# Four graph layers on one core: source keys first, masks on two engines, ranking by one scan per 32 columns

## What is computed

```
edge_index = stack([src, dst])
x = layernorm(x + segment_sum(h[dst], src))          # layer 0: h = x @ W.T + b
x = layernorm(x + layer1(x))                         # agg = segment_sum(h[src], dst), then an MLP, norm, relu
x = layernorm(x + layer2(x))                         # agg = segment_sum(weight * x[dst], src), two BN stages
x = layernorm(x + attention(x, edge_attr_128))       # softmax over the edges of one src
```

## Time and profile before

| | us |
|---|---|
| time, median of 3 runs | 6961.44 (6958.57 to 6962.66) |
| span of the profiled execution | 5494.9 |
| difference of the two | 1466.5 |
| GpSimd busy | 3860.8 (70% of the span) |
| VectorE busy | 3566.7 (65%) |
| TensorE busy | 3536.2 (64%) |
| ScalarE busy | 1431.3 (26%) |
| scatter DMAs issued (800) | from 108.3 to 1147.3 |

### The profile page before, as it was taken

One profiled execution on the slowest core, in us unless ns is written; L12 is line 12 of the kernel. 1 busy time (PEld: TensorE's weight loads), 2 busy tenths in 40 slices (PEclk: granted clock), 3 DMA queues, 4 the chain that ended last, 5 costly groups with the idle time before them and its releaser, 6 DMA issues.

```text
span 5494.9 us, 71163 instructions
## 1 busy us (share of the span) xinstructions
PE 3536.2 (64%) x14107; PEld 2622.1 (48%) x14107; DVE 3566.7 (65%) x11740; ACT 1431.3 (26%) x4459; POOL 3860.8 (70%) x4043
## 2 busy tenths in 40 slices
PE   2878694135555555566666656566666578888887
PEld 2655462024444444455555534444444445555554
DVE  8888887335555555566666645555554667788887
ACT  0211110000000000000000022222224456777776
POOL 2777777777777777777777667777773077777774
PEclk8999896567778777888888878877778789999999
DMA  3323231023333333333333333333331133343334
GB/s 86 82 70 78 64 89 37 2 71 112 111 111 112 111 113 104 107 113 111 113 111 112 100 98 105 105 105 105 105 105 49 51 106 109 111 113 111 112 112 75
DMA packets 257376, 521.07 MB, mean 95 GB/s; under 512 B 88217, under 2 KB 128621, under 8 KB 257139
## 3 DMA queue, kind: packets, MB, share of 16 engines
q0 software_dynamic: 179984, 423.92, 27.6%
q1 hardware_dynamic: 77155, 94.66, 5.9%
HBM read 483.72 MB, written 34.57 MB: 94 GB/s over the span
## 4 chain that ended last, share of the span: by engine, by line
PE 36%; POOL 17%; DMA 17%; issue 12%; DVE 12%; ACT 4%; DVEq 2%; SPq 0%; ACTq 0%; POOLq 0%
PE ps L1213 21%; POOL ZT L690 12%; DMA ZT<-table,meta_src 9%; POOL rec_src L635 5%; DMA ZT<-table,meta_dst 5%; PE ps L1223 3%; PE ps L1208 3%; DMA ACC<-in_edge_attr 2%; DVE ZT L1695 2%; PE ps L1172 2%; PE ps L1228 2%; DVE meta_src L1730 2%; DVE X L2117 1%; PE ps L1380 1%; DVE meta_src L1733 1%
## 5 line engine op out<-in xcount | busy, mean ns | idle before, releaser
L690 POOL DMA_INDIRECT ZT<-table,meta_dst x1616 | 1542.1, 954 | 684.7 <-issue 337.8
L690 POOL DMA_INDIRECT ZT<-table,meta_src x1568 | 1485.0, 947 | 513.8 <-issue 323.0
L1213 PE MATMUL ps<-ZT,xT 128*128 128x256 f32 x4704 | 1528.3, 496 | 467.7 <-DMA ZT<-table,meta_src 309.9
L1213 PEld LDWEIGHTS ps<-ZT,xT 128*128 128x128 f32 x4704 | 1215.2, 261 | 789.2 <-issue 179.7
L1812 DVE TENSOR_TENSOR ACC<-ps,ACC 128x256 f32 x2352 | 997.9, 424 | 813.4 <-PE ps L1213 553.8
L635 POOL DMA_INDIRECT rec_src<-ZT x800 | 796.4, 995 | 329.2 <-issue 239.1
L1208 PE MATMUL ps<-ZT,sel_x 128*128 128x256 f32 x294 | 162.6, 652 | 700.4 <-DMA ZT<-table,meta_src 495.9
L2117 DVE SCALAR_TENSOR_TENSOR X<-X,corr,ps 128x256 f32 x832 | 397.7, 478 | 134.5 <-PE ps L1223 47.2
L1172 PE MATMUL ps<-ewW,xT 128*128 128x256 f32 x1600 | 454.5, 386 | 0.0
L1223 PE MATMUL ps<-ZT,xT 128*128 128x256 f32 x1664 | 403.9, 393 | 50.7 <-ACT xT L965 21.5
L1208 PEld LDWEIGHTS ps<-ZT,sel_x 128*128 128x128 f32 x294 | 65.8, 279 | 751.4 <-DMA ZT<-table,meta_src 283.6
(11 more groups left out here) (423 smaller groups left out, 4530.9 us busy)
## 6 DMA issues: line engine op xcount, KB each, us to landing
ACC<-in_edge_attr SPq DMA_DIRECT2D x200, 240.0 KB
ZT<-table,meta_dst POOLq DMA_INDIRECT x1616
ZT<-table,meta_src POOLq DMA_INDIRECT x1568
rec_src<-ZT POOLq DMA_INDIRECT x800
table<-X SPq DMA_DIRECT2D x98, 128.0 KB
table<-ZT SPq DMA_DIRECT2D x49, 128.5 KB
table<-z SPq DMA_DIRECT2D x12, 512.0 KB
out<-X SPq DMA_DIRECT2D x48, 128.0 KB
```

Of the source, the lines that this page charges most:

```text
L690: pool.indirect_dma_start(rows[:, s % depth, 0:width], None, table[layer], bass.IndirectOffsetOnAxis(ap=ids[:, s, 0:1].bitcast(I32), axis= ...
L1213: nc.tensor.matmul(slot_sum(j), sel[:, k % 2, j, :], ring[:, (2 + k) % RG * G + j, 0:D], start=True, stop=True).then_inc(sem["summed"], 1)
```

## The change

**Loads.** SP waits for one memset in place of five and loads the source keys first, under a semaphore of their own (`src_in`). The next-partition words, the destination keys and the weights come behind; the node rows `X` come in one DMA behind the small loads and the first four steps of edge features.

**Masks.** VectorE makes masks 0 to 26 (`MARKED`). GpSimd makes masks 27 to 49 (`RANKED` is 50: the last stands for the empty partitions), and ScalarE counts them (`count_marks`). The copies of keys and weights into the records move from VectorE to ScalarE (`copy_pay`, `copy_list`).

**Ranks.** For each round's 32 columns (`RN`), ScalarE copies 50 masks by 32 columns to floats, laid out tile by tile with one place ahead of each tile (`open_steps`). VectorE puts each tile's base in that place and scans the whole line of 50 x 33 = 1650 in one instruction; a row of bytes (`going`) that is 0 at the head of each tile starts the sum anew. The last place of each tile is the next round's base. A product with the masks and a sum over the tiles leave the ranks of 32 columns. There are 25 such rounds: the first ahead of the edge work, the others each behind a round of it. The destination keys keep the old way (`rank_dst`), which does not run on these inputs.

**First layer's rows.** A pair of tiles in each of the 25 rounds: TensorE turns them after the third step of a round and multiplies after the sixth, in PSUM banks 6 and 7.

```diff
+RN = SC * SG
+MARKED = 27
+RANKED = T + 1
...
+            sp.wait_ge(sem["zeroed"], 1)
+            load_row(key[0], a["src"], sem["src_in"])
+            sp.wait_ge(sem["zeroed"], 4)
+            load_row(key[1], a["dst"], sem["keys_in"])
+            load_row(weight_row, a["edge_weight"], sem["keys_in"])
...
+            load_attr(0, 0, AR)
+            sp.wait_ge(sem["pool_set"], 1)
+            sp.dma_start(X[:, 0:T - 1, :], a["x"][0:(T - 1) * P, :].rearrange("(t p) d -> p t d", p=P)).then_inc(sem["x_in"], 16)
...
+            pool.wait_ge(sem["bucket_ready"], 1)
+            for b in range(MARKED, RANKED):
+                pool.tensor_scalar(mask[:, b, :], bucket, float(b if b < T else NO_NODE // P), None,
+                                   ALU.is_equal).then_inc(sem["marked"], 1)
...
-                    if c % (SC * SG) == 0 and c // (SC * SG) in BLOCKS:
-                        pool.wait_ge(sem["record_ready"], BLOCKS.index(c // (SC * SG)) + 1)
+                    if c % RN == 0:
+                        pool.wait_ge(sem["record_ready"], c // RN + 1)
+                        pool.wait_ge(sem["pay_set"], 3 if c == 0 else 6)
...
+            def count_marks(b):
+                act.wait_ge(sem["marked"], b - MARKED + 1)
+                nc.scalar.activation(mask[:, b, :], mask[:, b, :], ACT.Copy,
+                                     accum_out=small[:, 0, b:b + 1]).then_inc(sem["counted"], 1)
+
+            def open_steps(i):
+                c = slice(i * RN, (i + 1) * RN) if isinstance(i, int) else bass.ds(i * RN, RN)
+                wait(act, sem["record_ready"], i)
+                nc.scalar.copy(steps[:, :, 1:RN + 1], mask[:, :, c]).then_inc(sem["step_ready"], 1)
...
-                with dve.Fori(0, T) as b:
+                with dve.Fori(0, MARKED if n == 0 else T) as b:
...
-            def rank_block(which, block, c0, c1):
-                base = (which * (len(BLOCKS) - 1) + block) * T
                 for b in range(T):
-                    wait(dve, sem["ranked"], base + b - 1)
...
-                    v.tensor_tensor_scan(run[b % 2][:, c0:c1], ones[:, 0:1].to_broadcast([P, c1 - c0]), mask[:, b, c0:c1],
-                                         small[:, 5, b:b + 1], ALU.mult, ALU.add).then_inc(sem["scanned"], 1)
...
+            def rank_src(i):
...
+                own = steps[:, :, 1:RN + 1]
+                dve.wait_ge(sem["step_ready"], i + 1)
+                step(1, v.tensor_copy(steps[:, :, 0], rank_base[:, :]))
+                step(2, v.tensor_tensor_scan(step_line, going, step_line, 0.0, ALU.mult, ALU.add))
+                step(3, v.tensor_copy(rank_base[:, :], steps[:, :, RN]))
+                step(4, v.tensor_tensor(own, own, mask[:, :, c], ALU.mult))
+                step(5, v.tensor_reduce(found_rows, own.rearrange("p t c -> p c t"), AX_X, ALU.add))
+                v.tensor_copy(rec_of[0][:, c], found_rows).then_inc(sem["record_ready"], 1)
...
             edge_round(0)
-            for block in range(1, len(RANK_AT)):
-                with dve.Fori(max(RANK_AT[block - 1], 1), RANK_AT[block]) as i:
-                    edge_round(i)
-                rank_src(block)
...
+            rank_src(1)
+            with dve.Fori(1, SITERS - 1) as i:
                 edge_round(i)
+                rank_src(i + 1)
+            edge_round(SITERS - 1)
```

More of the change, by code:

```diff
@@ L182, in ring_group_3, with edge_rounds, last_round @@
     return b, u * RG + k
[L185 to L189, removed]
+def edge_rounds(eng, edge_round):
+    edge_round(0)
+    with eng.Fori(1, SITERS - 1) as i:
         edge_round(i)
-    edge_round(end - 1, last=True)
+    edge_round(SITERS - 1)
+def last_round(i):
+    return isinstance(i, int) and i == SITERS - 1
 def each_batch(body, first=0, end=NB):
@@ L299, in gnn_program @@
         row_from = small[:, 3, :]
+        rank_base = small[:, 3:5, :].rearrange("p i t -> p (i t)")[:, 0:RANKED]
         one_hot = cslot[0:T, 0:SLOTS]
@@ L742, in _ @@
             nc.scalar.activation(a_relu, a_relu, ACT.Copy, scale=1.0 - SLOPE).then_inc(sem["w_ready"], 1)
+            for b in range(half, T):
+                count_marks(b)
+            act.wait_ge(sem["marked"], RANKED - MARKED)
+            act.wait_ge(sem["counted"], T)
+            open_steps(0)
             act.wait_ge(sem["ew_psum"], 2)
@@ L1173, in edge_z, with edge_round @@
                 mm.then_inc(sem["ez_psum"], 1)
[L1175 removed]
+            def edge_round(i):
                 for u in range(ES):
[L1178 removed]
+                    if not (last_round(i) and u == ES - 1):
                         turn_attr(i, u + 1)
                     edge_z(i, u)
[L1181 to L1188 removed]
+                    if u == 2:
+                        if isinstance(i, int) and i == 0:
+                            pe.wait_ge(sem["w_ready"], 3)
+                            pe.wait_ge(sem["x_in"], 48)
+                        first_columns(i)
+                    if u == 5:
+                        first_rows(i)
+            pe.wait_ge(sem["split_ready"], 2)
+            pe.wait_ge(sem["zeroed"], 7)
+            pe.wait_ge(sem["pool_set"], 1)
+            turn_attr(0, 0)
+            for i in range(SITERS):
+                edge_round(i)
+            pe.wait_ge(sem["y_used"], NJ)
             order_tiles(0)
@@ L1706, in rank_src @@
-            def rank_src(block):
-                rank_block(0, block, BLOCKS[block] * SC * SG, BLOCKS[block + 1] * SC * SG)
+                    link(v.tensor_tensor_scan(run[0], ones[:, 0:1].to_broadcast([P, COLS]), mask[:, b, :],
+                                              small[:, 5, b:b + 1], ALU.mult, ALU.add))
+                    link(v.copy_predicated(pos, mask[:, b, :], run[0]))
+                v.tensor_copy(rec_of[1], pos).then_inc(sem["record_ready"], 1)
+                dve.wait_ge(sem["record_ready"], SITERS + 1)
@@ L1753, in _ @@
             order_slots_3()
+            dve.wait_ge(sem["keys_in"], KEYS_IN)
+            dve.wait_ge(sem["x_in"], 48)
             tile_counts(1, 1)
-            bases()
+            bases(small[:, 5, :])
             with dve.If(read_order(dve) > 0):
```

248 lines of the change are left out of this document (136 added, 112 removed).

## The result

| measured together, each line in one set on one chip | kernel before, us | changed kernel, us | ratio, 95% interval |
|---|---|---|---|
| the result | 6960.0 | 6835.0 | 0.983 [0.981, 0.985] |
| both once more | 6947.6 | 6848.3 | 0.985 [0.982, 0.988] |
| both in a later set | 5501.7 | 5550.0 | 1.009 [1.007, 1.010] |

A forecast was written before the change was run, and what follows sets the result against it. GpSimd was taken as the bound: first scatter at 56, plus 1017 + 10 + 91 = 1118 us, puts the last at 1174 against 1147.3, +26. So 6961.4 + 26 = 6988 us, range 6955 to 7020 (8 in 10).

The forecast's parts named there:

- The base: Whole time: span 5494.9 us, with 1466.5 us up to the median left as they are; the forecast adds 26 to 6961.4.
- what VectorE saves after 108 is hidden: Scatter stage: GpSimd's first scatter and its pace over 800 set the end, so VectorE's later savings gain nothing.
- VectorE becomes the bound: Rival, rank rounds: over 20.6 us each, VectorE decides; at 24 us, 7070 us. Chance 0.10, shared with a late start.
- First scatter at 56: Start of the stage: shorter loads, masks and first ranks bring the first scatter 52 us sooner, bounds 50 to 73.
- the bound not chosen: GpSimd's masks at the start: 2.12 us each by the two-input price, so done at 58 and first scatter at 73.
- Hold of the scatters: Rank rounds: scan (2.9 us) and product (0.85 us) hold GpSimd's scatters, 3.8 us a round, 91 us over 24.
- does not grow: Rival, rank rounds: the hold does not lengthen with the instruction, 24 rounds cost 11 us, time 6908 us. Chance 0.17.
- only the scan holds: Rival, rank rounds: the product holds no scatter, 70 us instead of 91, 6967 us. Chance 0.18, including anything between.
- Scatter's own pace: GpSimd's scatters when not held: 1.273 us each, 0.97 and 0.30 of issue, 1017 us for the stage.
- VectorE idle over 100 us before the read-back: End of the stage: sign that the forecast is right, VectorE having finished its work before the scatters end.
- Nothing changes behind the read-back: After the scatter list is read back: everything behind 1150.49 is untouched and only moves with the stage's end.
- the forecast of +26 us: End of the scatters: last scatter at 1174 against 1147.3, carried unchanged into the whole time.

The follow-up runs named there:

- the second trace of the changed kernel: The changed kernel, unchanged, profiled once more, with stops: 6848.3 us; the kernel before took 6947.6 us.

## Why the prediction was wrong, by its own steps

**The base, and with it the bound: the step that failed.** "The profile has the span, 5494.9, and 1466.5 us lie between it and the median; no row shows them and I leave them as they are." They do not lie outside the span: in every later run the time is 2 us above the span of the same execution. The trace was of an execution without stops, the median of runs with them, and the prediction applied the bound of the first to the time of the second. Where the result was measured, "what VectorE saves after 108 is hidden" is false: GpSimd waits 497 us for edge sums in the kernel before (412 of them behind its first scatter), and what shortens the edge stage counts. The prediction took the end of the old blocks at 12 us of scatters and the new rank rounds at 91; measured at the edge steps, which are the path there, they are 152 and 58. By the trace alone this could not be seen, but a gap of 1466.5 us that no row explains was a reason to give this case a chance of its own, with the edge steps as the bound already in the kernel before. The rival "VectorE becomes the bound" asked only whether the changed kernel crosses a threshold, and put it on the slower side.

The other steps can be read where their premise holds, without stops:

- **First scatter at 56, bounds 50 to 73: it is 76.8.** GpSimd's mask was taken at 1.03 us, and measured 2.21; the bound not chosen (2.12) was the right one. The prediction's own text gives a 58 for that; TensorE's sum starts at 57.7. ScalarE's count was taken at 1.25 and is 0.87, with 0.18 more to read its sum out. The first rank round takes 11.2 us, not 8.2: the sum over the tiles, priced by a row of 800 elements side by side at 1.8, takes 2.98 when it walks rows with a stride, and 1.9 us are the bias split's, of which the prediction said that it "comes behind and costs nothing" (see the run with all masks on VectorE).
- **Hold of the scatters, 91 us: right, at 86.** The two scatters that meet a scan and a product are 86 us above the median over the 24 rank rounds. All 800 are 800 x (1072 - 958) ns = 91 us above it, against 800 x (995 - 969) = 21 before; the forecast had 91 + 10. The rivals "does not grow" and "only the scan holds" fall by the timeline of the rank round.
- **Scatter's own pace:** 958 ns in place of 969, 9 us less over 800, not foreseen. With 5.8 us of waits for edge sums behind the first scatter: 76.8 + 1102.5 = 1179.3, where 1174 was forecast (56 + 1118). That the two lie so near is in part luck: a start 21 us later than forecast against a stretch 15 us shorter.
- **VectorE idle over 100 us before the read-back: 64.2.** The longer sum, 24 x 1.2 = 29 us, and longer rounds. The edge steps end at 959, not 866.
- **Nothing changes behind the read-back: wrong by 15 us.** The span grows by 47.1 and the scatter's end only by 32.0. The gathers of the last layer, in a line that the change does not touch, without stops, before and then after:

```profile
L690 POOL DMA_INDIRECT ZT<-table,meta_dst x832: 942/946/1484, 4389.8 to 5439.7; - x167
```

```profile
L720 POOL DMA_INDIRECT ZT<-table,meta_dst x832: 952/957/1737, 4427.0 to 5485.7; - x167
```

Each takes 11 ns more, some 9 us over 832. The other 6 come up in the second layer, between its first gather (+31.1) and the third layer's (+37.1). I have no cause for either, and no run was made for it.

So without stops the forecast of +26 us stands against +32 at the end of the scatters and +48 in the time. The sign was right there and wrong where it was asked.

## What the runs showed of the hardware

- **Stops.** In some sets VectorE, ScalarE, TensorE and SP are held again and again in dense stretches (an edge round of 51.6 us where 23.7 are enough), GpSimd was not seen held in this stage, and the same kernel takes 26% longer (6948 to 5498 us). Stretches with little work for TensorE are nearly free of them: the edge steps' end to the memset of `ACC` takes 159 us with stops and 151 without. SP is held even at waits that are long met (up to 1.4 us each, where 0.03 is usual). The cause is open; that the recording takes part is untested. The Trainium skill (Runtime: NRT & Kernel Launch, "Instruction fetch mechanics") says that a taken branch out of the fetched pages makes an engine wait for its instructions. That does not fit here: round 0 is written out on every engine, and TensorE's rounds all are, yet in the second trace of the changed kernel the first steps of that round (VectorE's L1820) are 2.6, 2.6, 4.3, 12.7 and 10.0 us apart.
- **A held GpSimd DMA.** The same skill (SBUF — State Buffer, "Who interferes with whom") reports a probe in which tensor_tensor did not stall GpSimd's DMAs. Here the product, a TENSOR_TENSOR with both inputs in SBUF, stretches the scatter beside it from 0.96 to 1.97 us. The measurement decides: the indirect DMA of this kernel, which takes its row numbers from SBUF, is held by it.
- **Prices.** A GpSimd comparison of 800 floats into bytes takes 2.21 us, where VectorE's own takes 1.05 and makes the count too. A scan of 1650 takes 3.60 us. A sum of 50 rows over 32 columns with a stride takes 2.98 us, 1.9 ns an element, against 1.2 for the earlier trace rows's row side by side.

## What to carry to other kernels

Before a sum is built on a trace, compare the span with the time: here they are 2 us apart in one and the same execution, and a difference of 1466.5 us meant two conditions, so that the bound had to be asked for under both. Work that is spread in short pieces between an engine's steps can disappear in waits that are there anyway, while the same work in a block stands on the path; which of the two counts hangs on whether that engine has such waits. And a second engine for part of a row of work helps only if its own price is known: at 2.21 us a mask GpSimd finished behind VectorE, and its bias split, pushed behind the masks, fell beside VectorE's first ranks and made these longer.
